# Token-row sums for the last block, low parts in pairs and attention outputs ahead of the query folds in a fused decoder layer

## What is computed

```python
x = layernorm(x + attn(x))           # silu(q), silu(k), silu(v), causal linear attention, sigmoid gate, Wp
x = layernorm(x + xattn(x, ctx))     # 16 heads, queries through Wq and w_kc_q, rope, W_qr; softmax; w_kc_kv, Wo
x = layernorm(x + ffn(x))            # 32 experts, 8 chosen per token

def expert_step(acc, xs):            # over the 32 experts
    w_gu, w_d, c_e = xs
    g, u = split(x @ w_gu.T)
    h = silu(g) * u                  # 96 wide
    return acc + h @ w_d.T * c_e[:, None]
```

## Time and profile before

| what | value |
|---|---|
| median of three runs | 860.18 us (859.62 to 860.51) |
| the profiled execution | 858.95 us, span 857.2 us |
| TensorE busy (share) | 830.4 us (97%) |
| VectorE | 637.9 us (74%) |
| ScalarE | 280.0 us (33%) |
| GpSimd | 182.0 us (21%) |
| granted TensorE clock, mean | 0.995 |

### The profile page before, as it was taken

How to read it: one execution, slowest core, us unless ns; L and a number is a source line. 1 busy time by engine, 2 the same in 40 slices (tenths; PEclk the granted TensorE clock), 3 DMA queues, 4 the chain that set the end, 5 groups by cost and what they waited for, 6 DMA issues and landing times.

```text
span 857.2 us, 15916 instructions
## 1 busy us (share of the span) xinstructions
PE 830.4 (97%) x6312; PEld 666.5 (78%) x6312; DVE 637.9 (74%) x1395; ACT 280.0 (33%) x500; POOL 182.0 (21%) x152
## 2 busy tenths in 40 slices
PE   8999999999999999999899999999999999999995
PEld 6967678876887768876577878888888888887884
DVE  5677698899888998887867866666665657566586
ACT  5431252204432144311544423332422333232242
POOL 3036500563006620264512201200000000000120
PEclk9999999999999999999999999999999999999998
DMA  9310000100001000000220052201012021000011
GB/s 352 120 38 2 3 2 12 51 2 5 2 13 50 3 5 2 24 3 30 96 74 25 1 143 72 79 0 64 33 46 67 0 92 37 25 1 0 2 50 49
DMA packets 12836, 35.85 MB, mean 42 GB/s; under 512 B 1504, under 2 KB 2272, under 8 KB 12384
## 3 DMA queue, kind: packets, MB, share of 16 engines
q1 hardware_dynamic: 12768, 34.92, 11.8%
HBM read 30.26 MB, written 2.36 MB: 38 GB/s over the span
## 4 chain that ended last, share of the span: by engine, by line
PE 47%; DVE 4%; issue 1%; ACT 0%; POOL 0%; ACTq 0%; DVEq 0%
PE ps L256 14%; PE ps L258 14%; PE ps L257 14%; PE ps L1620 2%; PE ps L1611 1%; DVE su L541 1%; DVE h_lo L371 1%; DVE x2T_all L535 1%; PE ps L1594 0%; PE ps L634 0%; PE ps L1522 0%; DVE fst L506 0%; PE ps L1468 0%; POOL roped L778 0%; PE ps L324 0%
## 5 line engine op out<-in xcount | busy, mean ns | idle before, releaser
L778 POOL TENSOR_TENSOR roped<-prod 128x512 f32<-128x512 f32 x96 | 121.3, 1287 | 233.3 <-DVE prod L1105 233.3
L541 DVE TENSOR_TENSOR su<-sg,ps 128x512 f32<-128x512 f32 x96 | 65.9, 687 | 122.7 <-PE ps L258 119.5
L256 PE MATMUL ps<-y_hi,f_hi 128*128 128x512 f32 x384 | 151.2, 394 | 1.3 <-issue 1.3
L258 PE MATMUL ps<-y_hi,f_lo 128*128 128x512 f32 x384 | 149.5, 389 | 0.0
L257 PE MATMUL ps<-y_lo,f_hi 128*128 128x512 f32 x384 | 149.4, 389 | 0.0
L398 ACT ACTIVATE sg<-ps 128x512 f32<-128x512 f32 x96 | 57.3, 598 | 251.4 <-PE ps L258 251.3
L1105 DVE TENSOR_TENSOR prod<-ps,ropeq 128x512 f32<-128x512 f32 x192 | 118.7, 681 | 24.7 <-PE ps L258 22.5
L256 PEld LDWEIGHTS ps<-y_hi,f_hi 128*128 128x128 f32 x384 | 72.1, 188 | 16.8 <-issue 2.2
L257 PEld LDWEIGHTS ps<-y_lo,f_hi 128*128 128x128 f32 x384 | 72.1, 188 | 15.2 <-issue 0.5
L258 PEld LDWEIGHTS ps<-y_hi,f_lo 128*128 128x128 f32 x384 | 72.1, 188 | 15.1
L256 PE MATMUL ps<-xT_hi,a_hi 128*128 128x512 f32 x192 | 78.7, 410 | 3.7 <-DVE prod L1105 2.1
(11 more groups left out here) (178 smaller groups left out, 1328.0 us busy)
## 6 DMA issues: line engine op xcount, KB each, us to landing
cb<-routing SPq DMA_DIRECT2D x32, 256.0 KB
f_raw<-in_L_ffn_gate_up_proj SPq DMA_DIRECT2D x8, 768.0 KB, 6.3
f_raw<-in_L_ffn_down_proj SPq DMA_DIRECT2D x8, 384.0 KB, 7.3
xb<-in_x SPq DMA_DIRECT2D x4, 512.0 KB, 4.2
lq<-in_L_xattn_Wq SPq DMA_DIRECT2D x1, 2048.0 KB, 14.2
x2T_all<-in_L_xattn_Wo SPq DMA_DIRECT2D x1, 2048.0 KB, 12.0
x2T_all<-x2T SPq DMA_DIRECT2D x4, 512.0 KB, 3.3
roped<-in_L_xattn_w_kc_q SPq DMA_DIRECT2D x1, 1536.0 KB, 9.9
```

The lines of the kernel that those rows point to most:

```text
L256: pe.matmul(dst, l_hi, r_hi, start=first, stop=False, skip_group_check=check)
L258: return pe.matmul(dst, l_lo, r_hi, start=False, stop=last, skip_group_check=check)
L541: dve.tensor_tensor(su[:, k % 2], sg[:, k % 2], bank(2 * (k % 2) + 1), ALU.mult).then_inc(s_su, 1)
L778: pool.tensor_tensor(roped[:, 2 * (t % 4) + k], made(2 * t + k)[:, 0], made(2 * t + k)[:, 1], ALU.add)\
```

## The change

Three parts, in the words of the diff:

- The last two rounds of down steps of the last body (steps 18 to 23, both for block 3) give token rows: acc of block 3 is first transposed into banks 6 and 7 (sum_turned, at step 20), and dn_tokens adds to it with h as the stationary operand (128 tokens) and 256 feature columns of the weights moving. The last two accumulates and the last turn_out go. The high products wait for h_hi alone, and the last step signals two tiles at a time. Block 2's statistics are at step 21 and its scale at step 22. The last store is by tiles (0, 2) and (1, 3).
- In the last body the six low parts are at steps 3, 3, 4, 5, 5, 6. TURN_C is 12.
- In linear(0) both attention outputs stand after fold 9, folds 14 and 15 behind turn_x, and the copies follow; the wait for a_lo moves into slots 0 and 1.

```diff
-    f_lo_step = lambda w, last: 15 if w == 0 else 3 if last else 5
+    f_lo_step = lambda w: 15 if w == 0 else 5
-    X2_STEPS, LOGITS_STEP, ROUTE_STEPS, TURN_C = (2, 4), 5, (8, 8, 9, 9, 10, 10), 11
+    X2_STEPS, LOGITS_STEP, ROUTE_STEPS, TURN_C = (2, 4), 5, (8, 8, 9, 9, 10, 10), 12
+    LAST_F_LO = {3: (0, 1), 4: (2,), 5: (3, 4), 6: (5,)}
-    FINAL_BANKS = (4, 4, 4, 0)
+    FINAL_BANKS = (4, 4, 4, 6)
-    TURN_OUT_STEPS, STATS_STEPS, SCALE_STEPS, APPLY_STEPS = (15, 18, 21), (15, 18, 22), (16, 19, 23), (17, 20)
+    TURN_OUT_STEPS, STATS_STEPS, SCALE_STEPS, APPLY_STEPS = (15, 18, 21), (15, 18, 21), (16, 19, 22), (17, 20)
+    TOKEN_STEPS = range(6 * ROWS, 8 * ROWS)
...
-                sp.wait_ge(s_res_end, 2)
-                sp.dma_start(out[n, :, 2:4], res[:, n, 2:4]).then_inc(s_out, 16)
-                sp.wait_ge(s_res, TILES * n + 2)
-                sp.dma_start(out[n, :, 0:2], res[:, n, 0:2]).then_inc(s_out, 16)
+                for t in range(2):
+                    sp.wait_ge(s_res_end, t + 1)
+                    sp.wait_ge(s_res, TILES * n + t + 1)
+                    sp.dma_start(out[n, :, t:4:2], res[:, n, t:4:2]).then_inc(s_out, 16)
...
-                if (k - 4) % ROWS == 0 and (not first or k >= 4):
+                if (k - 4) % ROWS == 0 and (not first or k >= 4) and not (last and k - 4 in TOKEN_STEPS):
                     accumulate((k - 4) // ROWS)
...
+                    if last and w == 1 and k in LAST_F_LO:
+                        for part in LAST_F_LO[k]:
+                            f_lo_part(dve, w, g, part)
...
             if last:
                 lo(STEPS - 1)
-                final_norm(2, 1)
-                accumulate(NB - 1)
                 final_norm(3, 0)
...
+            def sum_turned():
+                pe.wait_ge(s_acc, it * NB + TOKEN_STEPS[0] // ROWS + 1)
+                for t in range(TILES):
+                    for m in range(KC):
+                        c = LAST * BT + t * P
+                        pe.matmul(final_sum(LAST)[:, t, m * P:(m + 1) * P], acc[:, m, c:c + P], ident[:],
+                                  start=t % 2 == 0 and m == 0, stop=False, is_transpose=True, skip_group_check=True)
+            def dn_tokens(k):
+                w, n, j = place(k, first, last)
+                end = k == STEPS - 1
+                row = slice(GU + j * D, GU + (j + 1) * D)
+                def high(t):
+                    h = h_hi[:, k % 3, t * P:(t + 1) * P]
+                    for f in (f_hi, f_lo):
+                        pe.matmul(final_sum(LAST)[:, t], h, f[:, w, row], start=False, stop=False, skip_group_check=True)
+                def low(t):
+                    return pe.matmul(final_sum(LAST)[:, t], h_lo[:, k % 3, t * P:(t + 1) * P], f_hi[:, w, row],
+                                     start=False, stop=end, skip_group_check=True)
+                pe.wait_ge(s_hhi, base + k + 1)
+                for t in range(2 if end else TILES):
+                    high(t)
+                pe.wait_ge(s_hlo, base + k + 1)
+                for t in range(TILES):
+                    if end and t >= 2:
+                        high(t)
+                    mm = low(t)
+                    if end and t % 2 == 1:
+                        mm.then_inc(s_ft, 1)
...
-                dn(STEPS - 2)
-                dn(STEPS - 1)
-                turn_out(3)
+                dn_tokens(STEPS - 2)
+                dn_tokens(STEPS - 1)
...
-            for k in range(16):
+            for k in range(14):
                 a_hi_out(k)
...
+            xT_hi_out(b, 0, s_x1t, s_x1hi)
+            xT_hi_out(b, 1, s_x1t, s_x1hi)
+            a_hi_out(14)
+            a_hi_out(15)
             bdT_out(b, 0)
             bdT_out(b, 1)
-            xT_hi_out(b, 0, s_x1t, s_x1hi)
-            xT_hi_out(b, 1, s_x1t, s_x1hi)
...
-            for k in range(8, 12):
-                a_lo_out(k)
+            a_lo_out(8)
+            a_lo_out(9)
             residual1(b, 0)
-            a_lo_out(12)
-            a_lo_out(13)
             residual1(b, 1)
             norm1(b)
-            a_lo_out(14)
-            a_lo_out(15)
+            for k in range(10, 13):
+                a_lo_out(k)
             xT_lo_out(b, 0, s_x1hi, s_x1lo)
             xT_lo_out(b, 1, s_x1hi, s_x1lo)
+            for k in range(13, 16):
+                a_lo_out(k)
...
-            fold_a(8, 12)
+            fold_a(8, 10)
             pe.wait_ge(s_const, 3 * 16)
             attn_out(b, 0)
-            fold_a(12, 14)
             attn_out(b, 1)
+            fold_a(10, 14)
+            fold_u()
+            turn_x(b, 0, s_x1, s_x1t)
+            turn_x(b, 1, s_x1, s_x1t)
             fold_a(14, 16)
-            fold_u()
...
-            turn_x(b, 0, s_x1, s_x1t)
-            turn_x(b, 1, s_x1, s_x1t)
-            pe.wait_ge(s_alo, PAIRS * KC)
-            pe.wait_ge(s_tables, 4 * 16)
-            pe.sem_inc(s_kept, 1)
...
+                if b == 0 and t == 0:
+                    pe.wait_ge(s_alo, PAIRS * KC - 2)
+                if b == 0 and t == 1:
+                    pe.wait_ge(s_alo, PAIRS * KC)
+                    pe.wait_ge(s_tables, 4 * 16)
+                    pe.sem_inc(s_kept, 1)
```

More of the change, by code:

```diff
@@ L530, in accumulate @@
                 dve.wait_ge(s_acc, it * NB + nb + 1)
[L531 to L535, removed]
+                a = acc[:, :, cols(n)]
+                dve.tensor_tensor(a, a, ps[:, 6:8, :], ALU.add).then_inc(s_acc, 1)
             for k in range(STEPS):
@@ L554, in body @@
                 for w, g in ((1, 2 * it + 1), (0, 2 * it + 2)):
-                    part = k - f_lo_step(w, last)
-                    if 0 <= part < F_PARTS and not first and not (last and w == 0):
+                    part = k - f_lo_step(w)
+                    if last and w == 1 and k in LAST_F_LO:
+                        for part in LAST_F_LO[k]:
+                            f_lo_part(dve, w, g, part)
+                    if 0 <= part < F_PARTS and not first and not last:
                         f_lo_part(dve, w, g, part)
@@ L568, in body @@
                     final_norm(STATS_STEPS.index(k), 0)
-                if last and k in SCALE_STEPS[0:2]:
+                if last and k in SCALE_STEPS:
                     final_norm(SCALE_STEPS.index(k), 1)
@@ L619, in dn @@
                 mm.then_inc(s_d, 1)
+            def sum_turned():
[26 more added lines that the diff above has]
+                        mm.then_inc(s_ft, 1)
+                if not end:
+                    mm.then_inc(s_d, 1)
             def turn_out(n):
@@ L625, in turn_out @@
                     pe.wait_ge(s_res, TILES * n)
-                if n == LAST:
-                    pe.wait_ge(s_su, base + STEPS - 1)
                 f = FINAL_BANKS[n]
                 for t in range(TILES):
-                    if n == LAST and t == 2:
-                        pe.wait_ge(s_acc, it * NB + NB + 2)
                     for m in range(KC):
@@ L635, in turn_out @@
                                           acc[:, m, c:c + P], ident[:])
-                    if t == TILES - 1 or n == LAST and t == 1:
-                        mm.then_inc(s_ft, 1)
+                mm.then_inc(s_ft, 1)
             for k in range(STEPS):
@@ L641, in body @@
                     ffn_up(pe, it, k, first, last)
-                    dn(k - 2)
+                    if last and k - 2 == TOKEN_STEPS[0]:
+                        sum_turned()
+                    if last and k - 2 in TOKEN_STEPS:
+                        dn_tokens(k - 2)
+                    else:
+                        dn(k - 2)
                 if first and k in X2_STEPS:
```

## The result

| what | before | after |
|---|---|---|
| median of the runs timed side by side | 859.90 us (859.07 to 860.51, 4 runs) | 853.42 us (853.30 to 854.46, 4 runs) |
| profiled execution, span | 858.95 us, 857.2 us | 853.30 us, 851.3 us |
| TensorE busy | 830.4 us (97%) | 830.5 us (98%) |

The ratio is 0.993, 95% interval 0.9918 to 0.9942: 0.7% faster. The forecast was 853.9 with a range of 852.8 to 856.3. By the profiled executions the saving is 5.65 us, by their spans 5.82 (857.17 to 851.35), by the medians 6.5, against 6.25 forecast. The executions save less than the spans because what lies outside the span took 1.8 us before and 2.0 after. The total is close; the terms are less so, and two of them were wrong in opposite directions.

A forecast was written before the change was run, and what follows sets the result against it. TensorE, busy 97% of the span, was taken as the bound, so only gaps between its matmuls and the two ends could pay. 2.05 + 0.63 + 1.33 + 2.24 = 6.25 us off 860.18 gave 853.9, range 852.8 to 856.3.

The forecast's parts named there:

- three gaps: TensorE waits: 1.62 us ahead of the query products, 0.63 in the first expert body, 1.33 ahead of last-body step 9.
- the tail: After the last up product, a serial stretch of about 15 us; statistics there were to come 3.20 us earlier.
- (a): Rival, chance 0.12: the change in linear(0) gives nothing, so 855.9 us, or 854.9 with half of it.
- (b): Rival, chance 0.07 with lesser exposure: token matmuls cost their 0.19 us load, 5.1 us more, 859.0.
- (c): Rival, chance 0.04: load and stream do not overlap in token matmuls, 0.28 us spacing, 11.8 us more, 865.7.
- (d): Rival, chance 0.05: the 1.33 us ahead of step 9 is instruction issue, not the low part's wait; 855.2 us.
- The start: In linear(0), earlier attention outputs bring the first query product to about 48.45 from 50.50: 2.05 us saved, bounds 1.0 and 2.3.
- the margin of 0.2 us: In linear(0), TensorE's own work was to end at 48.2, 0.2 us ahead of the first query product.
- The routing: First expert body: transposes at step 12 instead of 11 no longer wait for VectorE, 0.63 us saved, bounds 0 and 0.7.
- The low parts: Last body: six passes end at step 6 instead of 8, so the whole 1.33 us wait goes; bounds 1.1 and 1.4.
- The token rows: Block 3's sums by token rows, steps 18 to 23: 3.20 + 0.15 - 1.11 = 2.24 us saved, bounds 1.5 and 2.6.
- The store: Last store, issued earlier but in 1 KB instead of 2 KB pieces: 0.15 us saved, bounds -0.3 and +0.35.

The follow-up runs named there:

- the start alone: The kernel before with only the change in linear(0) and slots 0 and 1: 857.49 us median, ratio 0.9973.
- the two extra passes: The kernel before with two more low-part subtractions in step 8 of the last body, ahead of the sixth low part: 863.28 us, one run.
- waiting first: The changed kernel, but a token step waits for h_lo before its first high product as well: 855.35 us median.
- the four parts: Four kernels, each the kernel before with one part: start 857.49 us, low parts 857.82, routing a step later 859.11, token rows 857.69.

## Why the prediction was right, point by point

**What bounds the kernel** was read rightly: three gaps and the tail, and the three gaps closed. What each gave came through to the end of the span, since TensorE does not pause for long elsewhere from the first expert product on (0.40 and 0.15 us in the first body). None of the rivals held: (a) by the start alone, (b) and (c) by the 0.12 us of the token matmuls, (d) by the two extra passes.

**The start**, 2.05 forecast and 2.02 measured (1.8 alone). The schedule worked out pass by pass was within 0.1 us at each point of VectorE and ScalarE. TensorE's was not: turn_x was to start at 45.1 and started at 45.33. The forecast had fold_u hold TensorE for 3.46 us, but in both traces the transposes behind it start 3.66 us after its start (42.92 to 46.58 before, 41.67 to 45.33 after). That took up the margin of 0.2 us, and TensorE became the last itself. What holds those transposes is not shown.

**The routing**, 0.63 forecast, 0.58 in the ledger. Read closely around the turn it is 0.68: what is saved rises from 1.95 us at the first up product of step 11 (490.55 before) to 2.63 at that of step 14 (504.41 before).

**The low parts**, 1.33 forecast, 1.51 to 1.58 measured. The mis-sized term is the idle row taken as the price. The idle counts from the modelled end of the last matmul, 0.39 us after its start, while the next would have started 0.227 after it; and the first matmul behind a wait is some 0.09 slower to hand over (0.31 us from 779.43 to 779.74 where the rhythm is 0.227, and at the transposes of the earlier trace rows, where the forecast did add it, 0.32 from 808.87 to 809.19). 1.33 + 0.16 + 0.09 = 1.58. The same rule gives what waiting first cost, if the changed kernel's own loss at that place is taken off: 0.85 idle, 0.16 (0.28 less 0.12) and 0.10 for the restart (0.22 instead of 0.12 to the next matmul) are 1.11, less the 0.14 below is 0.97, and 0.98 was measured. It does not settle every wait: for the routing's idle of 0.63 it would give 0.88, and the ledger of the steps around it gives 0.68. There, too, a restart is left: with the turn a step later, the first down product behind step 12's up products starts 0.34 ahead of the next one instead of 0.23 (497.84 and 498.18, in the kernel with that change alone).

**The token rows**, 2.24 forecast, 1.6 to 1.7 measured. Up to the last up product -1.15 for -1.11: right. The tail 3.04 for 3.20: the statistics start 3.99 us behind down step 21, where the forecast had 3.79. Most of that is in the rows: the first low product of step 22 starts at 841.49, 0.17 behind the last high one at 841.32 instead of 0.12, and its step hands over at 842.06 where an even rhythm gives 841.92. The forecast had h_lo done 0.07 ahead of the low products. It was done at 841.44 (840.75 and one pass of 0.69), just when they were due: a wait of 0.05 that the view is too coarse to list, and 0.09 for the restart. The rest lies ahead of the statistics, which start 0.11 behind the end of tile 1's last low product (842.93) and not 0.04. The store is the term with the wrong sign: +0.15 forecast with a lower bound of -0.3, -0.25 measured. The forecast saw the 1 KB pieces and priced them too low: its 0.15 was the author's estimate, and no row stands behind it.

**The median** fell by 6.5, more than the 5.8 of the spans. The rest is probably not the change's: of the four runs of the kernel before two were at 860.18 and 860.51, of the changed one's one was at 854.46 with a mean clock of 0.994 (the others 0.995). In the 31 runs of the kernel before beside the four parts, all thirteen from 860.11 up have a mean clock of 0.993 and all those up to 859.25 have 0.994 to 0.997, so the upper kind fits the long low clock, though no trace of the kernel before, as it stands, has the long stretch.

That the total came out so near is in part luck. Two terms were off by more than 0.1 us: the low parts gave 0.25 us more than forecast and the token rows 0.60 less. Together the terms were 0.43 too high against the spans (6.25 for 5.82). The scatter of the medians then added 0.66 the other way, so that on the median the saving of 6.48 lies 0.23 above the forecast. The forecast of 853.9 is 0.48 above the measured 853.42: 0.23 of it is that, and the rest is that it was taken from the earlier median of 860.18, which was 859.90 side by side.

## What to carry to other kernels

Price a TensorE wait at its idle plus the difference between one matmul's duration and the rhythm of its stream, plus the slow restart; here that was 1.58 for an idle of 1.33, and it held for a second wait and was too high for a third. A wait made longer can cost more than its own length: 0.94 us more of it here brought 1.6 us of the lower clock. Where a product is split into parts with different operands, let each part wait for its own operand alone: that was worth 1 us of the 3 in the tail. When two orders of a kernel differ by under 2 us, look at the granted clock in every stretch first, and fill a hole before comparing them.

## What the runs showed of the hardware

- Token matmuls of 256 columns with a fresh 128x128 load each start 0.12 us apart, those of 128 columns 0.11. A load shows as 0.19 us, longer than either, and the loads of the token steps start 0.12 apart as well: the load for the matmul at 839.16 starts at 839.05, together with the matmul before its own, and the next load at 839.17. So the records of full-height loads lie over those of running full-height matmuls, and over one another, without a wider spacing.
- A stretch with TensorE busy for about a third of its time (1.0 to 1.2 of 3 us) was followed by the lower clock, 0.50 of full speed, for a stretch that differed from one execution to the next (back at 1.00 by 416 us, or at 0.50 up to 418.5); the long kind cost 1.3 to 1.6 us, the short kind under 0.1. With six dummy matmuls in the holes the clock was 1.00 from 410 to 419 us.
- In the last body an idle of 1.33 us left the clock at 1.00 (779 to 785 us), and one of 2.27 us was followed by 0.50 of full speed (783 to 785 us; 0.57 over the next 3 us), with the 512-column matmuls 0.43 us apart instead of 0.23.
- 512 KB stored in pieces of 1 KB ran at 330 to 360 GB/s, in pieces of 2 KB at 360 to 400. The two issues took 1.34 us instead of 0.80. Issuing the 2 KB pieces from two queues at once instead of one made the end no earlier (6.61 us from the last aggregation, 6.60 with one).
